# A 32x32 factorization rewritten row by row, and the last part of an output chain moved beside the next group's assembly

## The chip, the cores and the metric

The kernel runs on one core of one Trainium2 chip. The metric is the device time of one execution in microseconds (us). Three runs of the kernel before gave 1550.6, 1553.78 and 1558.36 us, so their median is 1553.78. The profile that is read below is of one further execution, which took 1559.69 us; its span from the first to the last instruction is 1557.9 us.

## The reference, cut to what matters

The layer has an attention part and a feed-forward part over 16 sequences of 512 tokens with 128 features. The attention part works on 16 sequences x 16 heads x 4 chunks of 128 tokens, that is 1024 problems, and each of them solves a 64x64 ridge system:

```python
def step(S, qkv):
    Qc, Kc, Vc = qkv
    G = Kc.T @ Kc + RIDGE_EPS * I          # 64 x 64, one for each sequence, head and chunk
    W = jnp.linalg.solve(G, Kc.T @ Vc)
    U = U0                                 # the first 8 columns of the identity
    for _ in range(POWER_K):               # 2 rounds
        U, _ = jnp.linalg.qr(W @ U)
    Wr = U @ (U.T @ W)
    S_new = DECAY_ALPHA * S + Wr
    return (S_new, SCALE * (Qc @ S_new))
```

The output of the attention part is projected by Wo, scaled and added to the input. The feed-forward part then quantises its inputs in blocks of 16 to a 4-bit grid, and does gate, up and down projections.

## The kernel before

A front pass of about 140 us normalises the input and stores, for each sequence, its chunk covariances and what the main pass reads later. The main pass, which this change touches, handles the 16 sequences in G = 4 groups of 4. A group has 256 problems of 64x64, which lie two to a partition for VectorE (so its operands begin with 128 partitions x 2).

The 64x64 inverse is made by halves. For each group, in this order:

- **gram_stage and lead_extract** (together `feed`) build the matrices on TensorE and turn the leading 32x32 blocks into the problem layout, in which each partition holds whole matrices. ScalarE copies every PSUM bank out.
- **lead** on VectorE calls `factor` on the leading blocks. `factor` (from line 1556, its instructions on lines 1577 to 1636) eliminates one column after another, in place, and leaves the inverse of the triangular factor scaled by the square roots of the pivots, which GpSimd takes in three parts (`roots`, line 1485).
- **lead_return and schur** on TensorE bring the factor back (`from_problems`, transposes on line 807), form the Schur complement by small matrix products (lines 825, 835, 841) and extract it (`to_problems`, line 796).
- **schur** on VectorE calls `factor` on the Schur blocks.
- **schur_return and assemble** on TensorE bring that factor back (line 807 again) and put the full inverse together (lines 825, 835, 841), copied by ScalarE into `pair`.
- **subspace** on TensorE does two rounds of products with W and its transposes. Then **orthogonalise** on VectorE makes the 8 vectors orthogonal, with `lengths` on GpSimd (line 1509).
- **output** on TensorE projects on the basis and applies Wo and the queries. Its last part, from the transposes of xc and xa on line 1002 over the decayed sums on lines 1011 and 1016 to the products with the tokens on line 1028, yields the attention output in xc. ScalarE signals each sequence with y_out.
- **combine** on GpSimd (lines 1492, 1494) scales xc and adds the base, which SyncE loads for one sequence at a time in `tail` (lines 1384, 1385), and SyncE stores the sum.

The order is written out by hand, on each engine. VectorE runs, for g = 0, 1, 2: schur(g), lead(g+1), orthogonalise(g). TensorE and ScalarE run `walk(g)`, which is schur_return(g), assemble(g), subspace(g), lead_return(g+1), schur(g+1), and then output(g) woven with feed(g+2); for g = 2 there is no feed left and output runs alone. `woven` alternates two generators in proportion to the PSUM banks ("units") that each has done. TensorE fills 8 PSUM banks in a ring, and ScalarE empties them in the same order. GpSimd runs roots of lead(g+1), lengths(g), roots of schur(g+1), combine(g). The first two groups lie in a hardware loop (`Fori`), the third is a copy behind it.

After the last Schur factor, VectorE goes on with the inputs of the feed-forward part (`hidden.vector`), and GpSimd makes combine(2) after the second of these inputs' square roots (`hidden.pool`). SyncE loads the feed-forward weights only after the stores of combine(2); TensorE's `turn_rows` (line 743) waits for them.

A step j of the old `factor`, for j below 16, negates the column in two pieces (line 1592), clears the diagonal (line 1606), and then updates three areas ("near", "left", "right") of the matrix by an outer product (line 1577) and a sum (line 1585) each; above 16 it updates two areas. Line 1589 inverts the next pivot, and line 1617 clears the rest of a column.

## Time and profile before

| what | us |
|---|---|
| median of three runs | 1553.78 |
| the profiled execution | 1559.69 |
| its span | 1557.9 |
| TensorE matmul busy | 982.2 (63%) |
| TensorE weight load busy | 790.3 (51%) |
| VectorE busy | 1306.0 (84%) |
| ScalarE busy | 639.4 (41%) |
| GpSimd busy | 229.3 (15%) |
| line 1577, outer products of the factor, 608 instructions | 311.5 |
| line 1585, their sums, 608 instructions | 302.3 |
| mean granted TensorE clock, as a share of full speed | 0.828 |

The table is an average over stages that differ. The front pass ends at about 140 us, the four groups' attention work takes from there to about 1149 us, and the feed-forward part, beside the last group's attention, the rest. In the views, PE is TensorE's matmul queue, DVE VectorE, ACT ScalarE, POOL GpSimd, SP SyncE. A time in brackets behind a line is how long the engine sat idle before it, and the name behind the arrow is what ended that idle time. L807 is line 807.

### The profile page before, as it was taken

The page shows a single profiled execution, that of the slowest core. Times are in us where ns is not written, and L with a number is a line of the kernel's source. Part 1 is how long each engine was busy: PE and PEld are TensorE (multiplying, and loading weights), DVE is VectorE, ACT ScalarE, POOL GpSimd, SP SyncE. Part 2 cuts the span into 40 slices and gives each one's busy share as a digit, 9 for nine tenths or more (in the row PEclk, how much of TensorE's full clock was granted, in tenths as well). Part 3 has the DMA queues.
Part 4 walks back from the last instruction along what each step waited for, and adds up shares of the span by engine and source line. Part 5 has one row for each costly group of instructions (what it writes and reads, how often), then busy time and mean ns, then how long its engine had stood idle before and what let it go on. Part 6 is the DMA issues. An engine that isn't in the chain of part 4 may idle for free.

```text
span 1557.9 us, 44171 instructions
## 1 busy us (share of the span) xinstructions
PE 982.2 (63%) x17726; PEld 790.3 (51%) x17726; DVE 1306.0 (84%) x3841; ACT 639.4 (41%) x1294; POOL 229.3 (15%) x149
## 2 busy tenths in 40 slices
PE   1433920389077699776699876774446927797175
PEld 1333510365067567666567766673334725575064
DVE  5885579849999869999869999879884798878997
ACT  3563610256035366544356543342223513463142
POOL 3552001100201101312101302101231000003000
PEclk9975965689579899979799988888677978798597
DMA  2555010001000001110001110003013010111000
GB/s 74 169 182 185 21 35 0 1 23 48 0 4 3 4 3 51 33 66 3 4 4 50 33 53 3 3 10 109 2 42 97 17 56 17 48 45 31 8 18 29
DMA packets 52093, 61.69 MB, mean 40 GB/s; under 512 B 4048, under 2 KB 32416, under 8 KB 51888
## 3 DMA queue, kind: packets, MB, share of 16 engines
q1 hardware_dynamic: 51888, 58.84, 12.1%
q8 instruction: 142, 2.33, 0.6%
q14 instruction: 63, 0.52, 0.1%
HBM read 38.31 MB, written 20.51 MB: 38 GB/s over the span
## 4 chain that ended last, share of the span: by engine, by line
DVE 44%; PE 20%; issue 19%; POOL 4%; ACT 2%; DMA 1%; DVEq 1%; SPq 0%; POOLq 0%; ACTq 0%
DVE a_blocks L1585 11%; DVE a_outer L1577 10%; PE a_bank L835 3%; DVE a_blocks L1592 3%; PE a_bank L768 2%; POOL a_root L1485 2%; DVE a_recip L1589 2%; PE a_bank L697 2%; PE a_bank L825 2%; PE a_bank L841 2%; PE a_bank L796 2%; PE a_bank L786 1%; PE a_bank L807 1%; DVE a_work L465 1%; DVE a_work L462 1%
## 5 line engine op out<-in xcount | busy, mean ns | idle before, releaser
L1577 DVE TENSOR_TENSOR a_outer<-a_blocks 128x512 f32<-128x512 f32 (+19 forms) x608 | 311.5, 545 | 11.7
L1585 DVE TENSOR_TENSOR a_blocks<-a_blocks,a_outer 128x512 f32<-128x512 f32 (+19 forms) x608 | 302.3, 530 | 0.8
L1085 ACT ACTIVATE a_work<-a_bank 128x512 f32<-128x512 f32 (+1 forms) x193 | 110.9, 599 | 234.2 <-PE a_bank L807 197.9
L1485 POOL TENSOR_TENSOR a_root<-a_recip,a_half 128x32 f32<-128x32 f32 (+2 forms) x24 | 91.6, 3818 | 717.3 <-DVEq L1600 710.5
L807 PE MATMUL a_bank<-a_ident,a_blocks 128*128 128x128 f32 x256 | 42.5, 344 | 187.9 <-DVE a_blocks L1636 187.9
L807 PEld LDWEIGHTS a_bank<-a_ident,a_blocks 128*128 128x128 f32 x256 | 41.0, 209 | 189.4 <-DVE a_blocks L1636 134.8
L1085 ACT ACTIVATE a_solve<-a_bank 128x512 f32<-128x512 f32 (+2 forms) x184 | 88.0, 524 | 112.4 <-PE a_bank L841 52.1
L697 PE MATMUL a_bank<-a_wk,a_cg 128*128 128x512 f32 x256 | 117.6, 603 | 0.0
L1085 ACT ACTIVATE a_scaled<-a_bank 128x512 f32<-128x512 f32 (+1 forms) x130 | 65.6, 530 | 110.7 <-PE a_bank L825 72.3
L768 PE MATMUL a_bank<-a_scaled,a_blocks 128*128 128x352 f32 x256 | 88.4, 485 | 31.6 <-ACT a_scaled L1065 17.9
L825 PE MATMUL a_bank<-a_solve,a_work 32*32 32x64 f32 x4096 | 57.6, 241 | 64.4 <-issue 54.2
L835 PE MATMUL a_bank<-a_solve,a_minus 128*128 128x256 f32 x256 | 91.1, 518 | 1.2 <-issue 0.3
L825 PEld LDWEIGHTS a_bank<-a_solve,a_work 32*32 32x32 f32 x4096 | 47.9, 111 | 72.0 <-issue 70.6
L768 PEld LDWEIGHTS a_bank<-a_scaled,a_blocks 128*128 128x128 f32 x256 | 46.8, 195 | 56.7 <-ACT a_scaled L1065 18.4
L1085 ACT ACTIVATE a_xb<-a_bank 128x512 f32<-128x512 f32 x80 | 47.8, 598 | 63.8 <-PE a_bank L1016 23.1
L697 PEld LDWEIGHTS a_bank<-a_wk,a_cg 128*128 128x128 f32 x256 | 46.4, 191 | 50.5 <-issue 46.5
L1085 ACT ACTIVATE a_xa<-a_bank 128x512 f32<-128x512 f32 x96 | 54.7, 606 | 41.4 <-PE a_bank L923 19.5
L835 PEld LDWEIGHTS a_bank<-a_solve,a_minus 128*128 128x128 f32 x256 | 63.2, 259 | 16.4 <-issue 4.2
L1594 DVE TENSOR_SCALAR a_blocks<-a_blocks 128x64 f32<-128x64 f32 x8 | 1.8, 222 | 81.0 <-ACTq L1090 81.0
L354 PE MATMUL f_pt<-f_ident,f_xn 128*128 128x128 f32 x64 | 17.2, 421 | 80.5 <-DVE f_xn L401 80.5
L1592 DVE SCALAR_TENSOR_TENSOR a_blocks<-a_blocks,a_recip 128x28 f32<-128x28 f32 (+15 forms) x368 | 61.3, 194 | 5.3 <-DVE a_recip L1589 0.2
L1085 ACT ACTIVATE a_blocks<-a_bank 128x256 f32<-128x256 f32 (+1 forms) x94 | 42.0, 451 | 57.7 <-PE a_bank L786 23.4
(197 smaller groups left out, 2271.8 us busy)
## 6 DMA issues: line engine op xcount, KB each, us to landing
f_x<-in_L_attn_x SPq DMA_DIRECT2D x16, 256.0 KB, 3.2
s_xnt<-f_xt SPq DMA_DIRECT2D x16, 256.0 KB, 2.1
s_c<-f_cm SPq DMA_DIRECT2D x16, 256.0 KB, 2.3
s_base<-f_base SPq DMA_DIRECT2D x16, 256.0 KB, 2.8
a_cg<-s_c SPq DMA_DIRECT2D x16, 256.0 KB, 2.7
a_cc<-s_c SPq DMA_DIRECT2D x16, 256.0 KB, 3.6
a_xnt<-s_xnt SPq DMA_DIRECT2D x16, 256.0 KB, 3.7
a_base_in<-s_base SPq DMA_DIRECT2D x13, 256.0 KB, 2.6
```

The lines of the kernel that those rows point to most:

```text
L697: last = nc.tensor.matmul(bank[:], cg[bb % 2][:, 2 * (tp % 2) + i], wk[:, 8 * half:8 * half + 8, :].rearrange("p h d -> p (h d)"), start=T ...
L768: last = nc.tensor.matmul(bank[:, 0:FI], ht[:, t], w_gu[:, i], start=True, stop=True)
L796: last = nc.tensor.transpose(bank[:, i * P:(i + 1) * P], src[:, :, 4 * jb + i], ident[:])
L807: last = nc.tensor.transpose(bank[:, i * P:(i + 1) * P], rows_[:, :, 4 * rb + i], ident[:])
L825: last = nc.tensor.matmul(two[s][HB * c:HB * c + HB, i * DH:(i + 1) * DH], stationary(s, q), moving(s, q), start=True, stop=True)
L835: nc.tensor.matmul(four[c][:].rearrange("p (q z c) -> p q z c", z=2, c=HB)[:, :, half], mask[:], known[:, at:at + 8, :], start=True, stop= ...
L841: last = nc.tensor.matmul(four[c][rows(s, None), i * DH:(i + 1) * DH], both, both, start=False, stop=True, skip_group_check=True)
L1085: nc.scalar.activation(out, view, ACT.Copy, scale=scale).then_inc(emptied, 1)
L1485: nc.gpsimd.tensor_tensor(root[:, :, a:b], recip[:, :, a:b], half[:, :, a:b], ALU.pow).then_inc(roots_ok, 1)
L1577: return ch.inc(V.tensor_tensor(product, bcast(column, 2, area.shape[2]), bcast(row, 3, area.shape[3]), ALU.mult))
L1585: return ch.inc(V.tensor_tensor(area, area, product, ALU.add))
L1592: return ch.inc(V.scalar_tensor_tensor(out, src, -1.0, bcast(recip[:, :, j], 2, src.shape[2]), ALU.mult, ALU.mult))
```

## The change

`factor` is rewritten. Step j no longer updates the whole remaining matrix. It scales the known part of row i = j + 1 by the inverted pivots (weights), multiplies all later columns' known entries by it, sums these products along the innermost axis (`tensor_reduce`), and adds the sums to column i. The lower left part, which becomes the inverse, is updated by one outer product and one sum. A step has 8 instructions; the zeros of the other triangle are written at the end, in 31 memsets. Two small buffers are new, weight and total.

The last part of `output` becomes a function `write`. It no longer runs at the end of output(g), but woven with assemble(g+1), and `from_problems`, `assemble` and `solved` become generators for that. For the last group, write follows output as before. GpSimd's combine(g) moves behind the roots of lead(g+2); lengths(g+1) follows it. The hardware loop of TensorE and ScalarE becomes a Python loop, so its body is written out three times; the spare units that rounded the loop to the ring are gone. VectorE, GpSimd and SyncE keep their loops, and SyncE's order of transfers is the same.

```diff
 ROOTS = ((0, 16), (16, 28), (28, HB))
 LENGTHS = ((0, 6), (6, R))
...
+        weight, total = sb("weight", [P, 2, HB]), sb("total", [P, 2, HB])
...
-            def schur_return(self, g):
+            def assemble(self, g):
+
+
                 self.pe.wait_ge(schur_out, g + 1)
-                self.from_problems(3)
-                self.at["sback"] = self.u.mark()
-
-            def assemble(self, g):
-
-
-                self.u.need(self.at["sback"], apart=True)
+                m = yield from self.from_problems(3)
+                self.u.need(m, apart=True)
 
                 def scale(k):
                     return self.scale_rows(k, lambda s, q: work[rows(s, 1), q, :],
                                            lambda s, q: beside(kept[rows(s, 1), q, :], eyes[1][rows(s, 1)]))
 
                 marks = [scale(0)]
+                yield
                 for k in range(NQ // 32):
                     if k + 1 < NQ // 32:
                         marks.append(scale(k + 1))
...
                 self.pe.sem_inc(cc_used, 1)
                 m = yield from self.down_to_heads(wv, xb, m)
                 m = yield from self.up_to_model(wo, of_heads, m)
+                self.at["out"] = mp, m
+
+            def write(self, g):
+                mp, m = self.at["out"]
                 for buf, mark in ((xc, mp), (xa, m)):
                     self.u.need(mark)
                     for tb in range(T // 4):
...
                 yield from self.tiles(xb)
                 yield from self.heads(yb)
                 yield from self.model(xa)
+
+            def write(self, g):
                 yield from self.tiles(xc)
                 yield from self.tiles(xa)
...
 
-            e.schur_return(g)
-            e.assemble(g)
+            woven(e, (e.write(g - 1), WRITE_UNITS), (e.assemble(g), ASSEMBLE_UNITS))
             e.kept_free()
             steps = [("g", 0)] + [(kind, b + (kind == "g")) for b in range(B - 1) for kind in "gd"] + [("d", B - 1)]
             begin = steps.index(("d", 1)) + 1
@@ -1321,7 +1321,7 @@
             woven(e, (e.subspace(g), SUBSPACE_UNITS), (chain(e.turn_rows(), ffn(e, *steps[:begin])), 3 + units(steps[:begin])))
             e.wk_free()
             straight(ffn(e, *steps[begin:wait]))
-            woven(e, (e.output(g), OUTPUT_UNITS), (ffn(e, *steps[wait:end]), units(steps[wait:end])))
+            woven(e, (chain(e.output(g), e.write(g)), OUTPUT_UNITS + WRITE_UNITS), (ffn(e, *steps[wait:end]), units(steps[wait:end])))
             straight(ffn(e, *steps[end:]))
 
...
             e.lead_return(0)
             e.schur(0)
             straight(feed(e, 1))
-            start = e.u.n
-            with eng.Fori(0, G - 2) as g:
-                e.u.base = g * UNITS
-                walk(e, g)
-                woven(e, (e.output(g), OUTPUT_UNITS), (feed(e, g + 2), FEED_UNITS))
-            assert e.u.n - start == UNITS and UNITS % RING == 0
-            e.u.base = (G - 2) * UNITS
-            e.u.n = start
-            walk(e, G - 2)
-            e.grams_read()
-            straight(e.output(G - 2))
+            for g in range(G - 1):
+                if g == 0:
+                    straight(e.assemble(g))
+                else:
+                    woven(e, (e.write(g - 1), WRITE_UNITS), (e.assemble(g), ASSEMBLE_UNITS))
+                straight(e.subspace(g))
+                e.lead_return(g + 1)
+                e.schur(g + 1)
+                if g + 2 < G:
+                    woven(e, (e.output(g), OUTPUT_UNITS), (feed(e, g + 2), FEED_UNITS))
+                else:
+                    e.grams_read()
+                    straight(e.output(g))
             last_group(e, G - 1)
...
         APPLY_UNITS = 2 * (NQ // 32)
         FEED_UNITS = 3 * T + HB // 4
-        OUTPUT_UNITS = R // 4 + 3 * 4 + APPLY_UNITS + 3 * (T // 4) + 2 + NC + GB_N
+        OUTPUT_UNITS = R // 4 + 3 * 4 + APPLY_UNITS + T // 4 + 2
+        WRITE_UNITS = 2 * (T // 4) + NC + GB_N
         SUBSPACE_UNITS = 2 * (T // 4) + 2 * 2 + 2 * APPLY_UNITS + 4 + R // 4
-        SOLVE_UNITS = 2 * (NQ // 32) + NQ // 8 + HB // 4
-        UNITS = FEED_UNITS + OUTPUT_UNITS + SUBSPACE_UNITS + 2 * SOLVE_UNITS + HB // 4
-        SPARE = -UNITS % RING
-        UNITS += SPARE
+        ASSEMBLE_UNITS = HB // 4 + 2 * (NQ // 32) + NQ // 8
 
         LINKS = 2 * FACTOR_LINKS + 4 * R + 6 * (R - 1)
...
 
                 roots(1)
                 roots(2)
+                roots(3)
+                lengths(0)
+                roots(4)
                 with pool.Fori(0, G - 2) as g:
-                    roots(g * 2 + 3)
-                    lengths(g)
-                    roots(g * 2 + 4)
+                    roots(g * 2 + 5)
                     combine(g)
-                roots(G * 2 - 1)
-                lengths(G - 2)
-                roots(G * 2)
+                    lengths(g + 1)
+                    roots(g * 2 + 6)
                 hidden.pool(pool, 0)
                 hidden.pool(pool, 1)
...
-                    settled = ch.inc(V.tensor_scalar(diagonal, diagonal, RIDGE_EPS, None, ALU.add))
-                    inverse = pivot(0, settled)
-                    for j in range(HB):
-                        end = KEPT if j < KEPT else HB
+                    ch.link(V.tensor_scalar(diagonal, diagonal, RIDGE_EPS, None, ALU.add))
+                    inverse = pivot(0)
+                    for j in range(HB - 1):
+                        i, n_i = j + 1, HB - 1 - j
+                        row, rest = m[:, :, 0:j, j], m[:, :, 0:j, i:HB]
                         ch.wait(inverse)
-                        if j + 1 in (ROOTS[0][1], ROOTS[1][1]):
+                        if i in (ROOTS[0][1], ROOTS[1][1]):
                             dve.sem_inc(pivots_ok, 1)
-                        if j + 1 < HB:
-                            if j + 1 < end:
-                                column = negated(m[:, :, j, j + 1:end], m[:, :, j, j + 1:end], j)
-                            if j < KEPT:
-                                column = negated(m[:, :, j, KEPT:HB], m[:, :, KEPT:HB, j], j)
-                            cleared = ch.inc(V.memset(m[:, :, j, j], 0.0))
-                            ch.wait(cleared)
-                            if j < KEPT:
-                                near = multiply(j, "near")
-                                left = multiply(j, "left")
...
+                        weights = ch.inc(V.scalar_tensor_tensor(weight[:, :, 0:i], m[:, :, i, 0:i], -1.0, recip[:, :, 0:i], ALU.mult, ALU.mult))
+                        column = ch.inc(V.scalar_tensor_tensor(m[:, :, j, i:HB], m[:, :, i:HB, j], -1.0, bcast(recip[:, :, j], 2, n_i), ALU.mult, ALU.mult))
+                        ch.wait(weights)
+                        terms = area(0, n_i, i)
+                        known = ch.inc(V.tensor_tensor(terms, m[:, :, i:HB, 0:i], bcast(weight[:, :, 0:i], 2, n_i), ALU.mult))
                         if j:
-                            ch.inc(V.memset(m[:, :, j:HB, j - 1], 0.0))
-                        if j + 1 < KEPT:
-                            inverse = pivot(j + 1, settled)
-                            add(j, "left", left)
-                            add(j, "right", right)
-                        elif j + 1 == KEPT:
-                            settled = add(j, "right", right)
-                            add(j, "left", left)
-                            inverse = pivot(j + 1, settled)
-                        elif j + 1 < HB:
-                            settled = add(j, "near", near)
-                            add(j, "left", left)
-                            inverse = pivot(j + 1, settled)
+                            ch.wait(column)
+                            step = area(2 * KEPT * KEPT, j, n_i)
+                            product = ch.inc(V.tensor_tensor(step, bcast(m[:, :, j, i:HB], 2, j), bcast(row, 3, n_i), ALU.mult))
+                        ch.wait(known)
+                        summed = ch.inc(V.tensor_reduce(total[:, :, 0:n_i], terms, op=ALU.add, axis=AX_X))
+                        if j:
+                            ch.wait(product)
+                            ch.inc(V.tensor_tensor(rest, rest, step, ALU.add))
+                        ch.wait(summed)
+                        ch.link(V.tensor_tensor(m[:, :, i:HB, i], m[:, :, i:HB, i], total[:, :, 0:n_i], ALU.add))
+                        inverse = pivot(i)
                     ch.wait(inverse)
                     dve.sem_inc(pivots_ok, 1)
-                    ch.wait()
+                    for i in range(1, HB):
+                        V.memset(m[:, :, i, 0:i], 0.0)
                     ch.link(V.memset(diagonal, 1.0))
                     dve.wait_ge(roots_ok, n * 3)
                     V.tensor_tensor(m[:, :, 0:KEPT], m[:, :, 0:KEPT], bcast(root[:], 2, KEPT), ALU.mult)
```

## Rows read from the trace of the kernel before

**Rows 1.** waits of TensorE: who waited for whom, total us, times, longest
```profile
PE a_bank L807 <- DVE a_blocks L1636: 187.9, 8, 88.3
```

**Rows 2.** timeline of TensorE, first transposes behind seven factors: start, busy, ..., idle before
```profile
426.80 3.46 PE L807 MATMUL a_bank<-a_ident,a_blocks 128*128 128x128 f32 x15 [40.15 <-DVE a_blocks L1636]
...
514.37 5.42 PE L807 MATMUL a_bank<-a_ident,a_blocks 128*128 128x128 f32 x32 [2.34 <-DVE a_blocks L1636]
...
651.23 3.84 PE L807 MATMUL a_bank<-a_ident,a_blocks 128*128 128x128 f32 x32 [2.01 <-DVE a_blocks L1636]
...
745.02 5.22 PE L807 MATMUL a_bank<-a_ident,a_blocks 128*128 128x128 f32 x24 [9.43 <-DVE a_blocks L1636]
...
883.55 3.87 PE L807 MATMUL a_bank<-a_ident,a_blocks 128*128 128x128 f32 x32 [1.48 <-DVE a_blocks L1636]
...
977.23 3.04 PE L807 MATMUL a_bank<-a_ident,a_blocks 128*128 128x128 f32 x13 [9.07 <-DVE a_blocks L1636]
...
1108.67 1.54 PE L807 MATMUL a_bank<-a_ident,a_blocks 128*128 128x128 f32 x6 [35.18 <-DVE a_blocks L1636]
```

**Rows 3.** timeline of VectorE, where two of the factors begin and end
```profile
338.84 0.22 DVE L1594 TENSOR_SCALAR a_blocks<-a_blocks 128x64 f32<-128x64 f32 x1 [21.38 <-ACTq L1090]
...
425.97 0.68 DVE L1636 TENSOR_TENSOR a_blocks<-a_blocks,a_root 128x512 f32<-128x512 f32 x1
...
560.91 0.23 DVE L1594 TENSOR_SCALAR a_blocks<-a_blocks 128x64 f32<-128x64 f32 x1 [12.55 <-ACTq L1090]
...
649.20 1.75 DVE L1636 TENSOR_TENSOR a_blocks<-a_blocks,a_root 128x512 f32<-128x512 f32 x1
```

**Rows 4.** stretches: length, then PE, PEld, DVE, ACT, POOL busy; clock, DMA
```profile
651.20:692.00 40.80, 30.71 (x1088) 25.49 (x1088) 40.26 (x103) 14.57 (x28) 9.15 (x6) 0.75 0.28 93
692.00:735.60 43.60, 32.70 (x952) 30.06 (x937) 42.41 (x153) 21.77 (x41) 5.68 (x1) 1.00 0.01 3
...
793.50:882.10 88.60, 85.82 (x1002) 63.63 (x1000) 84.55 (x296) 56.98 (x117) 13.99 (x5) 1.00 0.08 24
```

**Rows 5.** VectorE groups by shape: count, busy us, mean ns, idle before
```profile
L462 DVE TENSOR_REDUCE a_work<-a_work 128x44 f32<-128x704 f32 x32 | 26.9, 881 | 0.5
...
L468 DVE TENSOR_TENSOR a_work<-a_work,a_outer 128x704 f32<-128x704 f32 x32 | 27.0, 886 | 0.0
...
L1592 DVE SCALAR_TENSOR_TENSOR a_blocks<-a_blocks,a_recip 128x32 f32<-128x32 f32 x128 | 27.0, 211 | 0.0
...
L1577 DVE TENSOR_TENSOR a_outer<-a_blocks 128x64 f32<-128x64 f32 x32 | 7.9, 266 | 0.8
...
L1617 DVE MEMSET a_blocks<- 128x62 f32 x8 | 0.9, 110 | 0.0
```

**Rows 6.** timeline of VectorE, first step of a factor, consecutive lines
```profile
339.67 1.16 DVE L1577 TENSOR_TENSOR a_outer<-a_blocks 128x960 f32<-128x960 f32 x1
340.86 1.16 DVE L1585 TENSOR_TENSOR a_blocks<-a_blocks,a_outer 128x960 f32<-128x960 f32 x1
341.94 0.69 DVE L1577 TENSOR_TENSOR a_outer<-a_blocks 128x512 f32<-128x512 f32 x1
342.54 0.16 DVE L1589 RECIPROCAL a_recip<-a_blocks 128x2 f32<-128x2 f32 x1
```

**Rows 7.** the last stretch, for lines 1002, 1011, 1016, 1028 alone
```profile
793.50:882.10 88.60, 4.04 (x32) 3.60 (x32) 1.00 0.08 24
...
793.50:882.10 88.60, 3.27 (x6) 0.90 (x6) 1.00 0.08 24
...
793.50:882.10 88.60, 4.32 (x32) 4.12 (x32) 1.00 0.08 24
...
793.50:882.10 88.60, 4.16 (x32) 3.81 (x32) 1.00 0.08 24
```

**Rows 8.** timelines of GpSimd and TensorE: combine(2) and turn_rows
```profile
1150.12 1.27 POOL L1492 TENSOR_TENSOR a_xc<-a_xc,a_ga 128x512 f32<-128x512 f32 x1
...
1181.95 1.43 PE L743 MATMUL a_bank<-a_ident,a_solve 128*128 128x128 f32 x6 [30.45 <-DMA a_solve<-s_wdn]
```

77 lines of the change are left out of this document (22 added, 55 removed).

## The prediction

> **What bounds the kernel now.** I read the waits of TensorE first. It sat 187.9 us, in 8 waits, until line 1636, the last instruction of a factor [rows 1]: once for every factor, 88.3 us for the first. So each factor's end releases TensorE. How much a shorter factor is worth depends on how long TensorE was idle before each release, and this is in the timeline [rows 2]: 40.15 us before 426.8 (first Schur factor), 35.18 before 1108.7 (last one), 9.43 and 9.07 before 745.0 and 977.2 (third and fourth lead), but only 2.34 before 514.4 (second lead) and 2.01 and 1.48 before 651.2 and 883.6 (second and third Schur factor). In the four groups the two engines are thus nearly balanced: a factor can give back only what TensorE idles behind it, unless TensorE's own share of that stretch also shrinks. This is what the second half of the change does.
>
> The stretches show TensorE's work [rows 4]. From 651.2 to 692.0 it assembles: 30.7 of 40.8 us busy, at a granted clock of 0.75, so 10.1 us idle in small gaps. From 692.0 to 735.6 runs subspace at full clock, and both together make 84.4 us. From 793.5 to 882.1 it does output and feed: 85.8 of 88.6 us busy, at full clock, so it is full.
>
> **The factor.** How long is it now? 338.84 to 426.65, 87.8 us, where nothing else disturbs it [rows 3]. The second Schur factor took 90.0 us, 560.91 to 650.95, with its last scaling at 1.75 instead of 0.68 us [rows 3]. The third lead factor went from there to 744.9, 94 us [rows 2, 3]. In both GpSimd was at work on combine, 9.15 us of the stretch behind 651.2 [rows 4], and I put the excess down to that.
>
> The price of one instruction: 128x704 takes 886 ns as a product and 881 as a reduction with 44 results [rows 5], 128x960 takes 1.16 us [rows 6]. A line through these is 0.15 us + 1.05 ns for each element of a partition. The starts [rows 6] give the spacing: 340.86 - 339.67 = 1.19 where the next instruction needs the result (duration + 0.03), 1.08 and 0.60 where it does not (duration - 0.08).
>
> The new step j, with i = j + 1 and n = 31 - j, has a known product and a reduction over 2·n·i elements each, and an outer product and a sum over 2·j·n each. Summed over 31 steps: 2·5456 twice and 2·4960 twice, 41664 elements, where the old factor has 54784. Terms:
> - 122 large instructions, all spaced by others: 122 x (0.15 - 0.08) + 41664 x 1.05 ns = 8.5 + 43.7 = 52.3 us
> - weights and column, 62 small ones of 0.21 us [rows 5], none waits for the one before: 62 x 0.13 = 8.1
> - the addition to column i, which the pivot needs: 31 x (0.18 + 0.03) = 6.5; the pivot's inverse, 0.16 us [rows 6], which the next step needs: 32 x 0.19 = 6.1
> - ridge 0.3; 31 memsets at the end of at most 110 ns each [rows 5], about 0.06 apart: 1.9; diagonal and the two scalings with the roots, as now: 2.1. GpSimd's third root now runs under the memsets, so its wait goes.
>
> The sum is 77.3, and I take **77.5 us**. The same rules applied to the old factor give 88.7 against 87.8 measured, so the method is good to about 1 us. Bounds: 75 if spacing of short instructions stays as tight as a memset's; upwards short runs count. Most sums in the new factor are over fewer than 16 elements, and no reduction like that is in the trace. A 128x64 product with short runs took 266 ns [rows 5], where the line gives 217: 49 ns more, which on 60 instructions makes 3 us, so 80.5.
>
> By the Trainium skill (VectorE: DVE Perf Modes, section Rules for kernel authors) a tensor_reduce on the hot path is the slowest VectorE operation and should be restructured away, which speaks against this change. In this trace the reduction of 704 elements is as fast as the product of 704 [rows 5]; by the row the sum stands, and by a reduction at half that rate it would be 11 us more a factor.
>
> **Where the factor's gain counts.** Segments of the span, before against after:
> - first lead, first Schur, last Schur factor: TensorE idles 88, 40 and 35 us behind them [rows 1, 2], so all of it counts: 3 x (87.8 - 77.5) = 30.9
> - second lead: TensorE's assemble(0) and subspace(0) end 2.34 us before it [rows 2]; there is nothing to write yet. Gain 2.3; TensorE is late next.
> - second and third Schur factor, 90.0 us each. Beside them TensorE did 88.6 us of output and feed [rows 4]. Write leaves it: its four lines cost 4.04 + 3.27 + 4.32 + 4.16 = 15.8 us [rows 7]. TensorE then needs 72.8, less than 77.5, so VectorE sets the end: 2 x 12.5 = 25.0. Without the move the gain here would be only the 1.5 to 2 us of idle time each.
> - third and fourth lead: the stretch from the Schur return to lead_return is 745.02 - 651.23 = 93.8 us, of which TensorE worked 84.4 [rows 2, 4]; the next group's is 93.7. Write comes on top, 15.8 us. The assembly's 10.1 us of gaps can take some of it in, since TensorE waits there for ScalarE (busy 14.6 of 40.8 us) and not for itself. I take 7 of 10: 84.4 + 15.8 - 7 = 93.2. VectorE's 77.5 is now far ahead. Gain 2 x 0.6 = 1.2. Bounds: nothing filled, and write at the low clock of this stretch (15.8/0.75 = 21): 105.5, a loss of 11.7 each; all gaps filled: 90.1, a gain of 3.7 each.
>
> **What is moved with it.** combine(g) now follows the roots of the next-but-one lead factor. That factor ends some 16 us before TensorE does, so combine (under 32 us with loads and stores, 1150.12 to 1181.95 for group 2 [rows 8]) meets the idle VectorE and the first half of orthogonalise. That is about 34 us, 514.4 to 560.91 less the 12.55 idle, so it has 12 us to spare beside lead_return and schur [rows 2, 3]: 0. The lengths that now queue behind combine on GpSimd are wanted only when six of its eight vectors are done: 0. SyncE's loads behind the later tail (the next group's cg, not needed before output(g+1)) and ScalarE's wait on `saved` have about 40 us: 0; if combine were 40 us late, each would cost what it is late. The last group is tighter: combine(2) began 41.5 us after the last Schur factor's return [rows 2, 8], held by the feed-forward input on VectorE, and turn_rows at 1181.95 waits on its stores [rows 8]. Write(2) now has its first signal after 13 of 16 of its units, 40 to 43 us into the weave; I charge 1.5. TensorE idled 30.45 us there, so write's own work is covered. Unrolling the loop removes a few register steps and adds instruction fetches; the second group, in the loop, and the third, already a copy behind it, took 93.8 and 93.7 us for the same stretch (651.23 to 745.02, 883.55 to 977.23 [rows 2]), so 0.
>
> **Sum**: 30.9 + 2.3 + 25.0 + 1.2 - 1.5 = 57.9 us. The profiled execution took 1559.7, so 1501.8 for one like it; it lies 5.9 us above the median of the three runs, and the forecast for the median is 1553.8 - 57.9 = **1496 us**.
>
> **The rivals.**
> 1. Write lands on TensorE's path undiluted. For it: assemble has its own waits in a fixed order, and a ring of 8 banks of which squares takes 4 at once. Against it: 10.1 us of gaps [rows 4]. The two stretches become 100 to 105 us: 14 to 24 us less gain, 1510 to 1520.
> 2. The denser stretch also raises TensorE's clock. The assembly ran at 0.75, between the levels 1.2 and 2.4 GHz, the dense stretches at 1.00 [rows 4]. The 30.7 us of work at full clock would be 5 to 8 us shorter in both: gain 10 to 16, 1480 to 1486. By the Trainium skill (TensorE: Matmul & The Clock Gate, section What's actually happening) the clock is throttled by default and activity releases it, which would make this the outcome; rows 4 agree as far as the dense stretch has 1.00.
> 3. The new factor is cheaper only by half: many short instructions, 83 us. Five factors lose 5.5 us each: 27 less, 1523.
> 4. Slower: each result of a reduction or each short run has a price of its own. A factor has 992 reduction results. Beyond 11 ns for each, the factor is 88.5 us, five exposed ones take back 55 us and the second lead 3, and the change costs from there on. At 15 ns: 92.4 us, 24 us slower, 1578. Against it: 44 results of 16 elements cost nothing over the line [rows 5].
> 5. The factor's gain does not arrive because TensorE becomes the bound everywhere (72.8 is really over 78 without write). Then the two Schur stretches give less, 5 us each: 1506.
>
> **How the numbers follow.** Chances: the forecast, with rival 5 in its width (1487 to 1509), 0.48; rival 1 0.18; rival 2 0.14; rival 3 0.12; rival 4 0.04; a new queue wait that eats all, 0.04. The likeliest case gives the time. The range goes from 1479 (rival 2) to 1526 (rival 3), which leaves out rival 4, the new wait and the ends. About 0.5%, 8 us, is what a measurement of this kernel can tell from no change: faster 0.92, same 0.03, slower 0.05.
>
> **What would show it.** The factor from line 1594's successor to its last scaling: 77.5 us in all eight calls, reductions of 2·n·i elements on the same line as products. The stretch beside the second Schur factor 78 us, with TensorE idle for about 5 at its end. The weave of write and assembly 50 us. lead_return without any wait for VectorE in the third and fourth group. combine after the lead factor's end, and the wait of turn_rows at its 30 us. Wrong would be the prediction if reductions lie above the line, if the weave takes over 60 us, or if VectorE waits for lengths.

## The result, and the profile after

The changed kernel takes **1483.63 us** (median of 4 runs, 1478.37 to 1489.35), where the kernel before took 1554.64 on the same chip (1550.6 to 1558.36): a ratio of 0.9532, 95% interval 0.9494 to 0.957. The forecast was 1496 in a range from 1479 to 1526. So the direction and the range held, but 71 us came where 57.9 were forecast. The profiled execution took 1489.35 us and its span is 1487.5, where before's was 1557.9; the 70.4 us between the two spans are what is to be found in the stretches. This execution is the slowest of the four, so its stretches are on the long side.

The first transposes behind seven factors on TensorE, which answer to [rows 2] (start, busy, idle time before in brackets; no bracket means no idle time; busy and the count x end where the window that was asked for ends):

```profile
404.46 5.72 PE L808 MATMUL a_bank<-a_ident,a_blocks 128*128 128x128 f32 x26 [30.09 <-DVE a_blocks L1595]
...
488.47 1.72 PE L808 MATMUL a_bank<-a_ident,a_blocks 128*128 128x128 f32 x14
...
609.81 3.68 PE L808 MATMUL a_bank<-a_ident,a_blocks 128*128 128x128 f32 x16 [5.26 <-DVE a_blocks L1595]
...
698.93 1.39 PE L808 MATMUL a_bank<-a_ident,a_blocks 128*128 128x128 f32 x6
...
821.66 3.68 PE L808 MATMUL a_bank<-a_ident,a_blocks 128*128 128x128 f32 x16 [5.25 <-DVE a_blocks L1595]
...
910.31 4.42 PE L808 MATMUL a_bank<-a_ident,a_blocks 128*128 128x128 f32 x32
...
1033.16 3.68 PE L808 MATMUL a_bank<-a_ident,a_blocks 128*128 128x128 f32 x16 [43.85 <-DVE a_blocks L1595]
```

Behind the three later lead factors (488.47, 698.93, 910.31) TensorE no longer waits: it is the late one. Behind the Schur factors it waits 5.26 and 5.25 us. The reader should see that the sides have changed places in the lead stretches. VectorE's timeline, where the second Schur factor and the third lead factor begin and end, against [rows 3]:

```profile
531.88 0.23 DVE L1563 TENSOR_SCALAR a_blocks<-a_blocks 128x64 f32<-128x64 f32 x1 [8.38 <-ACTq L1097]
...
609.07 0.68 DVE L1595 TENSOR_TENSOR a_blocks<-a_blocks,a_root 128x512 f32<-128x512 f32 x1
609.67 0.22 DVE L1563 TENSOR_SCALAR a_blocks<-a_blocks 128x64 f32<-128x64 f32 x1
...
688.02 1.75 DVE L1595 TENSOR_TENSOR a_blocks<-a_blocks,a_root 128x512 f32<-128x512 f32 x1
```

The first of the two takes 609.75 - 531.88 = 77.9 us, the other 689.77 - 609.67 = 80.1, with its last scaling at 1.75 us beside combine. Over all eight factors it is 77.5, 77.8, 78.0, 77.9, 80.1, 77.9, 80.1, 77.7. The stretches of TensorE that answer to [rows 4] (length, then PE, PEld, DVE, ACT and POOL busy with instruction counts, clock, DMA share, GB/s): lead_return and schur of the first pass, output and feed, the weave of write and assembly, subspace, and lead_return and schur of the next pass:

```profile
488.47:531.88 43.41, 32.41 (x1129) 27.69 (x1128) 30.52 (x77) 20.55 (x42) 3.28 (x2) 0.88 0.02 4
...
531.88:604.50 72.62, 71.93 (x908) 52.06 (x906) 70.20 (x239) 49.43 (x103) 9.59 (x2) 1.00 0.09 28
609.81:655.10 45.29, 41.67 (x1182) 35.99 (x1183) 43.80 (x147) 22.87 (x43) 5.43 (x1) 0.87 0.01 4
655.13:698.90 43.77, 33.18 (x938) 30.59 (x937) 33.12 (x136) 21.65 (x41) 11.71 (x6) 0.97 0.09 24
698.93:743.73 44.80, 33.89 (x1128) 29.44 (x1128) 33.78 (x76) 20.36 (x41) 9.06 (x6) 0.83 0.20 64
```

Output and feed fell from 88.6 to 72.6 us and is still full. The weave takes 45.3 us, only 4.5 more than the assembly alone did, and TensorE is busy for 41.7 of them.

Where the 70.4 us came from, by stretches between the start of a factor and the transposes behind it, before against after:

| stretch | before | after | gain | forecast |
|---|---|---|---|---|
| first lead, first and last Schur factor | 87.7, 88.0, 87.8 | 77.6, 77.9, 77.7 | 30.3 | 30.9 |
| second lead | 87.6 | 84.0 | 3.6 | 2.3 |
| second and third Schur | 90.3, 90.1 | 77.9, 77.9 | 24.6 | 25.0 |
| third and fourth lead | 93.8, 93.7 | 89.1, 88.7 | 9.7 | 1.2 |
| lead_return and schur, passes 0 to 2 | 46.5, 48.5, 43.7 | 43.4, 44.8, 45.1 | 5.4 | 0 |
| last return to turn_rows | 73.3 | 79.3 | -6.0 | -1.5 |
| all else | | | 2.8 | 0 |

Two rows carry nearly all of the miss: the third and fourth lead stretch, and the stretches of lead_return and schur, for which nothing was forecast. One sign that the forecast named did not appear: combine was to come behind the lead factor's end, and it begins at 685.7, 4 us ahead of it. The 80.1 us come from that, but they cost nothing, since TensorE needs until 698.9.

### The profile page after: what moved, and what is told of

Read it like the earlier page. It is cut to its first block, busy times and chain, and to the rows that moved or that the text cites. A ratio compares the mean times of both kernels' runs of the same rounds, so it can differ in the third digit from the quotient of the medians.

```text
span 1487.5 us, 43627 instructions
## 1 busy us (share of the span) xinstructions
PE 969.3 (65%) x17726; PEld 780.0 (52%) x17726; DVE 1230.2 (83%) x3729; ACT 640.3 (43%) x1294; POOL 231.3 (16%) x149
## 3 DMA queue, kind: packets, MB, share of 16 engines
q1 hardware_dynamic: 51888, 58.84, 12.6%
## 4 chain that ended last, share of the span: by engine, by line
DVE 36%; PE 32%; issue 13%; ACT 5%; POOL 2%; DMA 1%; SPq 0%; DVEq 0%; POOLq 0%; ACTq 0%
PE a_bank L840 5%; PE a_bank L830 3%; PE a_bank L846 3%; DVE a_total L1581 3%; DVE a_outer L1579 3%; DVE a_blocks L1584 3%; DVE a_outer L1575 2%; PE a_bank L946 2%; PE a_bank L961 2%; PE a_bank L769 2%; PE a_bank L898 2%; PE a_bank L698 2%; DVE a_blocks L1586 2%; DVE a_recip L1561 2%; PE a_bank L808 2%
## 5 line engine op out<-in xcount | busy, mean ns | idle before, releaser
L1575 DVE TENSOR_TENSOR a_outer<-a_blocks,a_weight 128x62 f32<-128x62 f32 (+15 forms) x248 | 129.4, 522 | 0.0
L1581 DVE TENSOR_REDUCE a_total<-a_outer 128x62 f32<-128x62 f32 (+30 forms) x248 | 127.0, 512 | 0.3
L1579 DVE TENSOR_TENSOR a_outer<-a_blocks 128x60 f32<-128x60 f32 (+14 forms) x240 | 119.2, 497 | 0.7 <-DVE a_outer L1575 0.7
L1584 DVE TENSOR_TENSOR a_blocks<-a_blocks,a_outer 128x60 f32<-128x60 f32 (+14 forms) x240 | 118.3, 493 | 0.0
L830 PE MATMUL a_bank<-a_solve,a_work 32*32 32x64 f32 x4096 | 54.3, 237 | 44.9 <-issue 38.4
L830 PEld LDWEIGHTS a_bank<-a_solve,a_work 32*32 32x32 f32 x4096 | 46.4, 110 | 48.7 <-issue 47.3
```

The source lines that it names most:

```text
L830: last = nc.tensor.matmul(two[s][HB * c:HB * c + HB, i * DH:(i + 1) * DH], stationary(s, q), moving(s, q), start=True, stop=True)
L1575: known = ch.inc(V.tensor_tensor(terms, m[:, :, i:HB, 0:i], bcast(weight[:, :, 0:i], 2, n_i), ALU.mult))
L1579: product = ch.inc(V.tensor_tensor(step, bcast(m[:, :, j, i:HB], 2, j), bcast(row, 3, n_i), ALU.mult))
L1581: summed = ch.inc(V.tensor_reduce(total[:, :, 0:n_i], terms, op=ALU.add, axis=AX_X))
L1584: ch.inc(V.tensor_tensor(rest, rest, step, ALU.add))
```

## The experiments

Each was run against the kernel before on the same chip. Ratios are compared, since the median of before differs a little between the chips (1554.3 to 1557.3). Where a ratio is turned into microseconds, it is times 1554.6.

### What each part is worth

**factor_only**: before with the new factor; order and loop as they were. All of `factor` is replaced, here its core:

```diff
-FACTOR_LINKS = 9 * HB + 6
+FACTOR_LINKS = 8 * (HB - 1) + 1
...
+                        known = ch.inc(V.tensor_tensor(terms, m[:, :, i:HB, 0:i], bcast(weight[:, :, 0:i], 2, n_i), ALU.mult))
...
+                        summed = ch.inc(V.tensor_reduce(total[:, :, 0:n_i], terms, op=ALU.add, axis=AX_X))
```

> The old order of the engines with the new factor alone. Theory (a factor gives back what TensorE idled behind it, and no more): first lead, first and last Schur factor 10.2 us each, second lead 2.3, the second and third Schur factor only their 2.0 and 1.5 us of idle time since output and feed still take 88.6 us, the third and fourth lead 9.4 and 9.1; about 55 us in all, so near 1500. In the stretch beside the second Schur factor TensorE is late and VectorE waits for nothing of it. Rival (the factor's gain counts in full wherever the chain of waits ran over it): 8 factors by 10 us or more, 80 us, so near 1475. Second rival (the move is what brings the Schur stretches their gain and the rest is small): 1520 or more.

Measured: 1501.54 us, ratio 0.964 (0.9602 to 0.9677), that is 56 us. The theory's number came. So the factor alone, with write still beside it, brings most of the gain.

**order_only**: the new order and the written-out passes with the old factor, the diff of the change without its part in `factor`.

```diff
+            woven(e, (e.write(g - 1), WRITE_UNITS), (e.assemble(g), ASSEMBLE_UNITS))
...
+            for g in range(G - 1):
```

> The new order with the old factor. Theory: beside the second and third Schur factor VectorE sets the end, 87.8 us now that combine no longer runs into its last scalings, 2.2 less each; the third and fourth lead factor (87.7 without combine beside it) end before TensorE's assembly with write and subspace (89 us), 4.7 less each; lead_return and schur of the next group 2 to 3 us less for the second and third group if their speed comes from TensorE not standing idle in front of them; the wait for the feed-forward weights 4 to 6 us longer. About 12 us less, near 1542. Rival (the move only shifts 15.8 us from one stretch to another, since TensorE is the bound in both): no change within 4 us.

Measured: 1544.52 us, 0.9932 (0.9903 to 0.9961), 10.6 us, near the theory's 12. With the old factor TensorE waits for VectorE behind every factor, 15 us behind the second and third Schur factor. The order can give little there.

**unroll_only**: before with TensorE's and ScalarE's passes written out.

```diff
-            with eng.Fori(0, G - 2) as g:
-                e.u.base = g * UNITS
-                walk(e, g)
-                woven(e, (e.output(g), OUTPUT_UNITS), (feed(e, g + 2), FEED_UNITS))
...
+            for g in range(G - 1):
+                walk(e, g)
+                if g + 2 < G:
+                    woven(e, (e.output(g), OUTPUT_UNITS), (feed(e, g + 2), FEED_UNITS))
```

> The kernel before with TensorE's and ScalarE's loop written out and nothing else changed. Lead_return and schur took 46.5 and 48.5 us in the looped groups before and 43.4 and 44.8 after the change. Theory A (the granted clock, after TensorE no longer idles 9 us in front of it): these two stay at 46 to 48 us, and the time at 1554 within 4 us. Theory B (waits against constants instead of registers, no branch): both fall to 44 us, and the time by 6 us or more.

Measured: 1549.86 us, 0.9964 (0.9945 to 0.9983), 5.6 us: near the border between the two expectations, and not nothing. The stretches of lead_return and schur did not decide it either. Before:

```profile
514.40:560.90 46.50, 35.11 (x1126) 30.23 (x1127) 30.28 (x76) 20.02 (x40) 3.28 (x2) 0.82 0.01 4
745.00:793.50 48.50, 36.45 (x1127) 31.43 (x1128) 30.34 (x77) 20.24 (x40) 3.28 (x2) 0.81 0.01 4
977.20:1020.90 43.70, 33.95 (x1120) 29.57 (x1120) 30.41 (x76) 20.24 (x40) 3.28 (x2) 0.87 0.01 3
```

The first two passes of unroll_only:

```profile
508.30:553.76 45.46, 36.38 (x1127) 31.36 (x1127) 30.37 (x76) 20.34 (x40) 3.28 (x2) 0.78 0.02 4
737.66:783.04 45.38, 36.79 (x1127) 32.12 (x1128) 30.38 (x76) 20.27 (x40) 3.28 (x2) 0.79 0.01 4
```

Their idle time fell, from 11.4 and 12.0 us to 9.1 and 8.6, but the busy time of the same matmuls rose by 1.3 and 0.3 us at a lower granted clock. Theory A had 46 to 48 us for them, theory B 44. Where more of it went is in TensorE's timeline, behind the third lead factor and the third Schur factor:

```profile
737.66 2.61 PE L807 MATMUL a_bank<-a_ident,a_blocks 128*128 128x128 f32 x11 [11.31 <-DVE a_blocks L1632]
...
873.10 5.27 PE L807 MATMUL a_bank<-a_ident,a_blocks 128*128 128x128 f32 x32 [2.71 <-DVE a_blocks L1632]
```

Before, these waits were 9.43 and 1.48 us [rows 2]. TensorE got faster and waited longer for the old factor. The five waits behind the second to the fourth lead and the second and third Schur factor are 6.5 us longer together.

**factor_unrolled**: factor_only and unroll_only together, so the whole change without the move of write and combine.

```diff
+            for g in range(G - 1):
+                walk(e, g)
...
+                        summed = ch.inc(V.tensor_reduce(total[:, :, 0:n_i], terms, op=ALU.add, axis=AX_X))
```

> The old order with the new factor, and TensorE's and ScalarE's loop written out: the changed kernel without the move of write and combine. The factor alone gave 1501.5, the written-out loop alone 5.6 us. Theory A (the three parts add up): 1496, and the move is worth the remaining 12 us, of which about 8 come from the two woven stretches. Theory B (the written-out loop matters more once TensorE is the bound in both stretches, since nothing hides its register steps): 1485 to 1490, and the move is worth little. The rows to look at are lead_return and schur of the second and third group: 47.7 and 47.9 us in the loop with the factor alone; 45 by both theories.

Measured: 1482.92 us, 0.9549 (0.9519 to 0.9579), 70.1 us. Theory B holds, and further than it went: this is the whole change's ratio (0.9532) within the intervals. Writing the passes out is worth 14 us here, from 0.964 to 0.9549, and the move of write and combine nothing that can be measured. (With the old factor the same comparison, order_only against unroll_only, gives 5 us, and those intervals overlap too.) The stretches of lead_return and schur show it. First factor_only, its two looped passes and then its copied pass:

```profile
488.81:536.74 47.93, 35.29 (x1129) 29.94 (x1128) 30.54 (x76) 20.55 (x42) 3.28 (x2) 0.79 0.01 4
713.46:761.18 47.72, 35.97 (x1129) 30.76 (x1128) 30.53 (x77) 20.54 (x42) 3.28 (x2) 0.79 0.01 4
933.52:975.42 41.90, 32.36 (x1122) 27.93 (x1120) 30.53 (x77) 20.55 (x42) 3.28 (x2) 0.88 0.02 4
```

Then factor_unrolled, its first two passes:

```profile
483.90:525.96 42.06, 32.86 (x1129) 28.07 (x1128) 30.53 (x77) 20.55 (x42) 3.28 (x2) 0.88 0.02 4
696.74:739.71 42.97, 33.52 (x1127) 29.57 (x1128) 30.38 (x77) 20.12 (x40) 3.28 (x2) 0.88 0.02 4
```

The same matmuls take 47.9 and 47.7 us inside the loop and 42 to 43 outside it in these two programs. TensorE's idle time falls from 12.6 to 9.2 us in the first pass (47.93 - 35.29 against 42.06 - 32.86), and its busy time by 2.4, at a granted clock of 0.88 where it was 0.79. Idle and busy time have to be kept apart. This is the third pass of scalar_unrolled (described below), which lies outside TensorE's loop too:

```profile
929.14:975.74 46.60, 37.35 (x1120) 32.19 (x1120) 30.38 (x77) 20.13 (x40) 3.28 (x2) 0.77 0.01 3
```

It is as long as some looped pass, at a clock of 0.77, and yet idles only 9.3 us. Over the fourteen traces the six looped passes took 46.5 to 48.8 us and idled 11.4 to 12.8 of them; the 36 written-out ones took 40.8 to 48.3 and idled 6.8 to 11.0. On average that is 12.1 us of idle time against 9.3, and this part of the loop's cost shows in every pass; the busy time varies with the clock by more than that, in loops and outside. Nor is this stretch all of it: between the two profiled spans (1505.1 and 1478.0 us) it has 10.6 us, the second and third lead stretches 3.6 and 3.4, the second and third Schur stretches 3.8 together.

**tensor_unrolled** and **scalar_unrolled**: the new factor and the old order, only one of the two engines with its passes written out.

```diff
-            with eng.Fori(0, G - 2) as g:
...
+            if isinstance(e, Tensor):
+                for g in range(G - 1):
+                    walk(e, g)
...
+            else:
...
+                with eng.Fori(0, G - 2) as g:
```

The second has `Scalar` in place of `Tensor`.

> The old order with the new factor, and only TensorE's loop written out; ScalarE keeps its loop. The factor alone gave 1501.5, with both loops written out 1482.9. Theory (the looped waits cost on TensorE itself, in the small matmuls of assemble and schur): 1483 to 1489; lead_return and schur of the second and third group 43 us, as with both written out. Rival (ScalarE's looped waits and flags delay the releases for which TensorE waits): 1497 to 1502 and 47 us. If both share it: near 1492.

> The mirror of the one before: new factor, old order, only ScalarE's loop written out, TensorE keeps its loop. Theory (the cost is TensorE's): 1497 to 1502, lead_return and schur at 47 us. Rival (the cost is ScalarE's): 1483 to 1489 and 43 us. Both together say whether the 18.6 us add up.

Measured: 1481.38 us, 0.9543 (0.9504 to 0.9581), for TensorE's, and 1497.6 us, 0.9621 (0.9587 to 0.9655), for ScalarE's. So the cost is TensorE's own loop; the first is just below its 1483 to 1489, the second within its 1497 to 1502. The two groups of waits that answer it, of tensor_unrolled and then of scalar_unrolled (who waited for what, total us, times, longest; "issue" is time in which TensorE waited for nothing that the profile shows):

```profile
PE a_bank L826 <- issue: 42.5, 25, 3.0
```

```profile
PE a_bank L826 <- issue: 55.0, 28, 3.5
```

Line 826 is the first of the small 32x64 products. In the loop each wait of TensorE on a bank of the ring compares with a value that depends on the pass, since `need` and `fill` count from `base = g * UNITS`. Written out, the value is a constant. That working out these values is the price fits the place and the engine, but the profile does not show such operations, and it was not tried alone, nor apart from the loop's branch.

### The place of write

**unwoven**: the change with write as one piece ahead of the assembly.

```diff
-                    woven(e, (e.write(g - 1), WRITE_UNITS), (e.assemble(g), ASSEMBLE_UNITS))
+                    straight(e.write(g - 1))
+                    straight(e.assemble(g))
```

> The changed kernel with write run in one piece ahead of the assembly, not woven with it. Theory (the weave both fills the gaps and raises the granted clock): write then costs its own 15.8 us and more for its waits on ScalarE, and the assembly its old 41 us at a clock near 0.8, so 57 to 60 us where the weave took 45.3; two of the three such stretches are exposed, 24 to 28 us in all, near 1508. In the last group the wait for the feed-forward weights covers it. Rival (the move to this place is what counts, the weave little): within 6 us of the changed kernel.

Measured: 1480.29 us, 0.9519 (0.9484 to 0.9554), so the rival held (within 6 us of the changed kernel), and my theory, that the weave is needed to fill the assembly's gaps, fell. The stretches of write and of the assembly behind it:

```profile
602.60:619.80 17.20, 13.33 (x94) 10.89 (x92) 16.17 (x96) 7.76 (x15) 1.64 (x1) 1.00 0.01 2
619.87:655.84 35.97, 29.09 (x1090) 24.03 (x1088) 34.97 (x103) 15.06 (x29) 5.43 (x1) 0.81 0.02 4
```

Write now starts ahead of the factor's end, which is at 607.8, in the 5 us in which TensorE would wait for it, and at full clock. After that the assembly takes 36.0 us, where before it took 40.8 [rows 4] inside the loop. Here too the loop had counted: factor_unrolled, with write still in its old place, has its assembly at 37.5 and 36.2 us. 5.2 us of cover and the assembly at its written-out price are as good as the weave.

**write_after**: write as one piece behind the assembly.

```diff
-                    woven(e, (e.write(g - 1), WRITE_UNITS), (e.assemble(g), ASSEMBLE_UNITS))
+                    straight(e.assemble(g))
+                    straight(e.write(g - 1))
```

> The changed kernel with write run in one piece behind the assembly. Ahead of it, write used 5.2 us of TensorE's idle time before the second and third Schur factor's end, and all of it fell into idle time before the last one; behind the assembly it can use none. Theory (weaving saves TensorE's gaps, and so does a place in idle time; the two came out equal only because both are of one size): write costs its 17.2 us whole, assembly and write make 53 to 58 us where the weave took 45.3, and the two exposed groups 16 to 26 us, near 1500 to 1508. Rival (neither place nor weave counts, since what is saved in the gaps comes back as a lower clock behind it): within 6 us of the changed kernel, 1478 to 1490.

Measured: 1516.3 us, 0.9725 (0.9693 to 0.9757): 30 us more than the change, and 8 more than its theory had. The two exposed stretches are 13.2 and 9.2 us longer, together inside the theory's 16 to 26; the last group adds 11.8, which it had not counted. The two together, from the factor's end on:

```profile
607.30:667.30 60.00, 47.82 (x1190) 40.26 (x1191) 58.18 (x189) 25.26 (x47) 5.43 (x1) 0.81 0.01 3
```

60.0 us stand against 45.3 in the weave: 12.2 idle against 3.6, and 6.2 us more busy at a clock of 0.81 instead of 0.87. Nothing fills the gaps and there is no cover from a factor. In the last group the late write also holds combine(2): turn_rows comes 91 us behind the last return (1051.5 to 1142.56) instead of 79.

### The end of the last group

The table shows 6 us lost between the last return and turn_rows. Combine(2) starts 41.8 us behind the return, as before (41.5), but its eight instructions took longer, 17.9 us instead of 13.0. GpSimd's timeline after, against [rows 8]:

```profile
1081.75 3.22 POOL L1492 TENSOR_TENSOR a_xc<-a_xc,a_ga 128x512 f32<-128x512 f32 x1 [4.15 <-DMA a_ga<-s_mod]
1085.05 3.19 POOL L1494 TENSOR_TENSOR a_xc<-a_xc,a_base_in 128x512 f32<-128x512 f32 x1
...
1099.77 1.26 POOL L1492 TENSOR_TENSOR a_xc<-a_xc,a_ga 128x512 f32<-128x512 f32 x1 [3.44 <-DMA a_ga<-s_mod]
1101.11 3.19 POOL L1494 TENSOR_TENSOR a_xc<-a_xc,a_base_in 128x512 f32<-128x512 f32 x1
```

The same scaling on line 1492 takes 1.26 or 3.22 us. What decides it is in VectorE's timeline. After:

```profile
1081.56 2.29 DVE L180 TENSOR_TENSOR a_solve<-a_solve,a_blocks 128x2048 f32<-128x2048 f32 x1
1083.88 3.23 DVE L181 TENSOR_TENSOR a_solve<-a_solve,a_blocks 128x2048 f32<-128x2048 f32 x1
```

Before, GpSimd's and VectorE's at the same place:

```profile
1157.67 1.26 POOL L1494 TENSOR_TENSOR a_xc<-a_xc,a_base_in 128x512 f32<-128x512 f32 x1
...
1157.71 3.37 DVE L180 TENSOR_TENSOR a_solve<-a_solve,a_blocks 128x2048 f32<-128x2048 f32 x1
```

After, GpSimd's instruction starts 0.2 us behind VectorE's line 180, has its remaining 2.1 us to sit out, and ends 1.1 us later; line 181 takes 3.23 us instead of 2.29. Before, it starts just ahead of line 180 and takes 1.26 us, and line 180 takes 3.37. So here the two do not run side by side: whoever comes second waits. Over all fourteen traces, each of the 91 combine instructions longer than 1.8 us lasts what VectorE's running instruction had left, plus 1.12 to 1.15 us; the 60 that met an idle VectorE take 1.26 to 1.30. A reduction does not hold GpSimd up: the 27 that began with more than 0.3 us of one still to run take 1.26 to 1.28 us. So the 6 us are for the most part (4.9) a matter of phase, of where combine's starts, which follow its loads, happen to fall on VectorE's instructions.

Four experiments ask what this end is worth if it is taken off the path.

**rows_early**: the change, with SyncE's loads of the feed-forward weights (`after_second`) ahead of the last three stores of combine(2).

```diff
                         if bb >= 1:
                             store(g, bb - 1)
+                        if bb == 1 and after_second:
+                            after_second()
```

> The changed kernel with SyncE's loads of the feed-forward weights put behind the second of the four base loads of combine(2), as soon as the assembly of the last group has freed their place, not behind its last store. Theory (the wait of turn_rows is set by combine(2) on GpSimd and lies on the path): the wait falls from 29 us to about 5, TensorE gets to the first gate 24 us sooner, and VectorE, which was idle 23.7 us before its first quantisation, follows from 1106 instead of 1130 us: 12 to 20 us less, 1464 to 1472. Rival (the end is set by VectorE's later work or by the last group's chain, and the wait has slack): 0 to 4 us.

Measured: 1458.96 us, 0.9381 (0.9353 to 0.941), 23 us below the change by the ratios, somewhat more than the 12 to 20 expected. The wait of turn_rows is 4.08 us, where it was 29.4:

```profile
1081.78 1.43 PE L744 MATMUL a_bank<-a_ident,a_solve 128*128 128x128 f32 x6 [4.08 <-DMA a_solve<-s_wdn]
```

**write2_early**: the change, with write(2) right behind output(2), ahead of the last Schur factor's end, and combine(2) one step earlier on GpSimd.

```diff
-            woven(e, (e.write(g - 1), WRITE_UNITS), (e.assemble(g), ASSEMBLE_UNITS))
+            straight(e.assemble(g))
...
                     straight(e.output(g))
+                    straight(e.write(g))
...
-                hidden.pool(pool, 1)
                 combine(G - 2)
+                hidden.pool(pool, 1)
```

> The changed kernel with write of the third group moved back behind its output, where TensorE idles 43.9 us beside the last Schur factor, and combine(2) put before the second input's square root on GpSimd, where GpSimd idles 30 us. Theory: the last assembly is unwoven and 4 to 6 us shorter; combine(2) runs from about 1042 us and ends near 1068, so the weights are loaded when the assembly ends, near 1078 instead of 1112; gain as for the early loads and 1 to 3 us more, 1461 to 1470. Rival (combine beside VectorE's first input slows both through their shared access, and the second input comes later by what is won): 0 to 5 us.

Measured: 1454.83 us, 0.9335 (0.9298 to 0.9371), the lowest of all and below its 1461 to 1470, though its interval overlaps that of rows_early: about 100 us below before and 30 below the change. TensorE idled 43.85 us ahead of that return, write(2) fits in it, and the return still has 25.9 us to wait:

```profile
1034.74 1.12 PE L808 MATMUL a_bank<-a_ident,a_blocks 128*128 128x128 f32 x4 [25.87 <-DVE a_blocks L1596]
...
1083.92 1.43 PE L744 MATMUL a_bank<-a_ident,a_solve 128*128 128x128 f32 x6 [6.28 <-DMA a_solve<-s_wdn]
```

**unwoven_combine**: unwoven, with the same step of GpSimd.

```diff
                 hidden.pool(pool, 0)
-                hidden.pool(pool, 1)
                 combine(G - 2)
+                hidden.pool(pool, 1)
```

> The unwoven kernel, write ahead of the assembly in one piece, with combine(2) before the second input's square root on GpSimd. Theory: as the one before it in the last group, since its write of the third group also lies in TensorE's idle time, and equal to the weave in the others: 1460 to 1470. Rival (the weave keeps its worth once the last group is the same in both): 5 us or more above the one before.

Measured: 1463.32 us, 0.9408 (0.936 to 0.9455), so combine's place alone brings 17 us to unwoven. That is within the theory's 1460 to 1470, but 11 us by the ratios above write2_early, as the rival had it (5 us or more), and their intervals just touch. Whether the weave keeps some worth in the other groups stays open.

**rows_and_write2**: write(2) early and the weights ahead of the second base load, with GpSimd's order as in the change.

```diff
-            woven(e, (e.write(g - 1), WRITE_UNITS), (e.assemble(g), ASSEMBLE_UNITS))
+            straight(e.assemble(g))
...
+                    straight(e.write(g))
...
+                        if bb == 0 and after_second:
+                            after_second()
```

> The changed kernel with two of the last group's edits together: write of the third group behind its own output, in TensorE's idle time, and the loads of the feed-forward weights ahead of combine(2)'s second base load; GpSimd's order as in the changed kernel. Theory (what the last group gains is bounded by VectorE's two inputs, which end 73 us behind the last Schur factor whatever TensorE does): the second input comes 6 us earlier than with combine in front of it, the weights 5 us earlier than before; 1450 to 1459, no more than 5 us from the better of the two. Rival (TensorE's time in the last group is on the path too): 1445 or less.

Measured: 1459.74 us, 0.9376 (0.9353 to 0.9399). This is at the upper end of the theory's 1450 to 1459 and 5 us above write2_early; the rival's 1445 or less fell. The two do not add, and the result is that of rows_early. Both remove the same wait, whose rest is 2.5 us here, so an early write(2) brings nothing beyond the early loads. What then sets the end is VectorE's first two inputs of the feed-forward part, in my reading of the timelines; that was not tried by itself.

## Why the prediction was right or wrong, point by point

- **What bounds the kernel** was right: each factor's end released TensorE, and five of the eight factors, those behind which it idled or whose beside work shrank, gave back 54.9 of the 55.9 us forecast for them.
- **The factor's price** was right: 77.5 was forecast and 77.5 to 78.0 measured in six calls, 80.1 in two. The two are beside combine, as the excess of before was put down to, and the traces bear that out: in every kernel a factor with two of combine's instructions beside it is 2 us longer, and one with six of them 5 to 6 us. The sum had its bound of 80.5 for short runs, and it was not needed. The groups of VectorE after, by shape (count, busy us, mean ns, idle before), answer to [rows 5]:

```profile
L1575 DVE TENSOR_TENSOR a_outer<-a_blocks,a_weight 128x384 f32<-128x384 f32 x16 | 8.8, 552 | 0.0
...
L1581 DVE TENSOR_REDUCE a_total<-a_outer 128x16 f32<-128x384 f32 x8 | 4.4, 545 | 0.0
L1581 DVE TENSOR_REDUCE a_total<-a_outer 128x48 f32<-128x384 f32 x8 | 4.4, 545 | 0.0
```

  The line of the prediction gives 0.15 + 0.40 = 0.55 us for 384 elements. The product has 552 ns, the reduction 545, with 16 results of 24 elements as with 48 of 8. So rivals 3 and 4 fell. By the Trainium skill (VectorE: DVE Perf Modes, section Rules for kernel authors) tensor_reduce on a hot path runs at 1x and is the slowest VectorE operation, and restructuring should be considered. In this case's fp32 rows it runs at the product's rate, so avoiding it had nothing to win here; the measurement decides.
- **Second and third Schur stretch**: 25.0 forecast, 24.6 measured. TensorE's output and feed without write took 72.6 us, where 72.8 was forecast, and idled 5.3 behind it, where about 5 was. Rival 5 fell.
- **Third and fourth lead stretch**: 93.2 forecast, 89.1 and 88.7 measured, 9.7 us of gain instead of 1.2. Here a term was mis-sized: the weave takes 45.3 us, where assembly and write at their own prices are 40.8 + 15.8 = 56.6. Of the 11.3 us between them the gaps gave 10.1 - 3.6 = 6.5, where I let them give 7. The other 4.8 are TensorE's busy time, 15.8 + 30.7 = 46.5 us before and 41.7 in the weave, at a granted clock of 0.87 instead of 0.75 [rows 4]. But 40.8 us is the price in the loop. The assembly of factor_unrolled, written out and without write (second and third group):

```profile
613.15:650.65 37.50, 29.69 (x1090) 24.57 (x1088) 36.47 (x111) 15.16 (x29) 7.99 (x6) 0.82 0.31 100
826.89:863.07 36.18, 28.70 (x1090) 24.11 (x1088) 35.16 (x108) 15.16 (x29) 8.39 (x6) 0.81 0.27 89
```

  Against these, 3.3 of the 11.3 us are the unrolling's. The weave itself saves 8.0 us in the first (4.2 of gaps, 3.8 of busy time) and 6.3 in the second, whose weave took 45.7 (3.6 and 2.7). Only the busy time is rival 2's mechanism, 3.8 and 2.7 us where it had 5 to 8. By the Trainium skill (TensorE: Matmul & The Clock Gate, section What's actually happening) activity releases a clock that is throttled by default; the trace agrees only so far, as the denser stretch has the higher clock but not 1.00. Rival 2's result of 1480 to 1486 came about, but by luck: its mechanism carries 6.5 us of it, and unwoven and factor_unrolled reach the same time without a weave. The forecast also read the gaps as waits for ScalarE. TensorE's waits between 651.2 and 692.0 of before say otherwise for most of them:

```profile
PE a_bank L825 <- issue: 7.2, 4, 2.0
PE a_bank L825 <- ACT a_work L1085: 2.6, 1, 2.6
```

- **Unrolling at 0** is the step that failed. I compared the second group (in the loop) with the third (its copy) over the stretch behind the Schur factor and found 93.8 and 93.7 us [rows 2]. That stretch ended, in both, with TensorE waiting 9.43 and 9.07 us for VectorE, so its length was the factor's. Taking the waits off does not help, though: TensorE's own part was 84.4 us in the loop and 84.6 in the copy. The copy's assembly and subspace, in the trace of before:

```profile
883.55:922.10 38.55, 29.56 (x1088) 24.51 (x1088) 38.03 (x97) 14.56 (x28) 8.87 (x6) 0.82 0.26 83
922.10:968.15 46.05, 36.97 (x941) 34.27 (x936) 44.81 (x162) 21.89 (x41) 5.67 (x1) 0.89 0.01 3
```

  Against the loop's 40.8 and 43.6 us [rows 4] the copy gained 2.3 in the assembly and lost 2.4 in subspace, where its clock was 0.89 instead of 1.00. That the lengths agree is chance; the idle time does not, 21.0 us in the loop and 18.1 in the copy. The same goes for lead_return and schur, where TensorE and ScalarE alone set the pace. In length they say little: 46.5 and 48.5 us in the loop, 43.7 in the copy, but 46.4 for the same work ahead of the first group, outside the loop, at a clock of 0.74:

```profile
292.41:338.84 46.43, 38.59 (x1122) 32.90 (x1123) 22.41 (x79) 20.03 (x40) 0.00 (x0) 0.74 0.05 15
```

  In idle time they are apart: 11.4 and 12.0 us in the loop, 9.7 and 7.8 outside it. Unrolling is worth 5.6 us with the old factor (unroll_only), where about half of it goes into waits, and 14 us with the new one (factor_unrolled against factor_only), nearly all of it TensorE's (tensor_unrolled).
- **What the move of write brings** was mis-stated with it. The prediction gave it the second and third Schur stretches (21 to 22 us of the 25.0). It did bring them 9.3 us each against factor_unrolled (87.2 to 77.9), but write came back in the lead stretches (83.6 to 89.1 and 83.7 to 88.7, 10.4 us), in lead_return and schur (127.0 to 133.3 us over three passes), and at turn_rows (72.6 to 79.3). In sum it is 0.9549 against 0.9532, which can't be told apart.
- **The moved queues**: the lengths were there in time, ScalarE's and SyncE's moved waits cost nothing that shows, as forecast. Combine beside lead_return and schur was put at 0; against factor_unrolled these stretches are longer by 1.4 us where nothing of combine is beside them, and by 1.8 and 3.2 where it is. Combine is not shown to be the cause: the 3.2 are busy time at a clock of 0.76 instead of 0.90 (36.2 us instead of 32.5), and the idle time there is 9.0 us instead of 9.5. At turn_rows 1.5 was forecast and 6.0 lost. The late signal of write(2) did not do it, since combine(2) starts 41.8 us behind the return as before. Its own instructions took longer, 17.9 us for 13.0, by the phase to VectorE's. In unwoven they ran at 1.26 to 2.12 us and turn_rows came 72.4 us behind. Why the phase falls so in one kernel and not in the other stays open.
- **The sum**: 57.9 forecast, 70.4 in the profiled spans. The excess is 8.5 in the lead stretches, 5.4 in lead_return and schur, 2.8 elsewhere and 0.3 in the factor-bound ones, less 4.5 at turn_rows: 12.5.

## What to carry to other kernels

To price a hardware loop, compare a looped pass with its copy by the engine's idle and busy time apart, with the granted clock beside them, and not by length. Here a wait for the other engine made two lengths equal, and with the wait taken off a lower clock in one part did so again; the idle time showed the difference in the trace of before. Once the slowest engine is made faster, small costs of the next one, such as the gaps inside a hardware loop, come onto the path. Before weaving two pieces of work together, look for idle time ahead of a release that one of them fits into: a straight write there was as good as the weave (unwoven). And ask what a store or a load at the end of a chain holds up: 17 to 30 us lay in the order of SyncE's and GpSimd's work in the last group, more than in the weave.
